# Slot and expert inputs turned for the matrix unit: one 128-column transpose for the last 64 features of two blocks

## Chip, cores and metric

The kernel runs on one core of a Trainium2 chip. The metric is the device time of one execution in microseconds (us): 1408.03 us is the median of three runs (1406.95 to 1409.55). The engines of the core are named as in the profile: PE is TensorE (PEld its weight loads), DVE is VectorE, ACT is ScalarE, POOL is GpSimd, and SP issues most transfers.

## The reference

A small language-model tower over 32 batches of 128 tokens with 192 features: embedding, attention, a soft mixture of 64 experts, attention with 12 heads, and a routed mixture of 8 experts. The change touches the inputs of the two mixtures:

```python
# soft mixture: x is [32, 128, 192], phi_n is [64, 16, 192]
logits = jnp.einsum('bmd,npd->bmnp', x, phi_n)
D = jax.nn.softmax(logits, axis=1)
C = jax.nn.softmax(logits.reshape(bsz, m, n * p), axis=-1)
Xs = jnp.einsum('bmd,bmnp->bnpd', x, D)
hdn = _layernorm(Xs, ln_g[:, None, :], ln_b[:, None, :])
hdn = jnp.einsum('bnpd,ndh->bnph', hdn, w1) + b1[:, None, :]   # h = 384
hdn = jax.nn.gelu(hdn, approximate=False)
Ys = jnp.einsum('bnph,nhd->bnpd', hdn, w2) + b2[:, None, :]
Y = jnp.einsum('bsd,bms->bmd', Ys.reshape(bsz, n * p, d), C)
# routed mixture: 8 experts of 512 tokens, h = 768
h = gelu(jnp.einsum('ecd,edm->ecm', expert_inputs, w1) + b1[:, None, :])
expert_outputs = gelu(jnp.einsum('ecm,emd->ecd', h, w2) + b2[:, None, :])
```

## The kernel before

The program has four phases, one after the other: `tower_phase` (embedding, attention, slot logits and slot sums; 0 to 340 us of the profiled span), `expert_phase` "e0" (the 64 experts of the soft mixture; 340 to 875 us), `combine_phase` (second attention and router; to about 1260 us) and `expert_phase` "e1" (the 8 routed experts; to the end).

Each expert works on 512 rows of 192 features, held as four blocks of 128 rows. The first product contracts over features, so the features must lie on the 128 partitions: PE turns each block with transposes against `ident`. 192 features are one full run of 128 and a rest of 64. The rest is laid out twice side by side (columns `D:` of `rows`, written by a DVE copy after the norm at L1379, or by a second transfer at L220 for the routed experts), so that a full 128-column transpose gives the 64 remaining features twice, in the lower and in the upper 64 partitions. That makes 8 transposes for an expert: four blocks times two.

fp32 operands are split into a high part (rounded to fp32r) and a low part. The high and low parts of the rest are stacked over the two halves of the partitions, `e_x_hi_over_lo`, so that the rest costs two products instead of three. After the transposes, ACT takes both turned banks to `e_x_full` (L1289, two of 128x512) and rounds both (L1295, one of 128x1024); DVE subtracts for the low part of the first 128 features (L1348) and makes the stack with a sign that is 0 in the lower and -1 in the upper half (L1350).

One turn of the e0 loop is, on PE: 15 matmuls of the first product for expert n (three output banks of five, L60 is the helper `matmuls`), the 8 transposes for expert n+2 (L1218), and 12 matmuls of the second product for expert n (L1246). Each fp32 matmul stands in the profile as two records, so the 12 are 24 records. They contract over the three parts of `h_full` in turn, and in the first block of rows PE waits ahead of the first, second and third matmul for the GELU of that part on ACT (L1319, counted by `acted`). On DVE a turn is: split of expert n+1, low part of its weights (L1355), layer-norm statistics of expert n+3 (L1362 to L1369), a wait for POOL's power (L1180), the norm (L1376, four of 128x192), the copy (L1379), and the bias addition of expert n (L1404), which waits for the second product. SP's loads wait for semaphores of these steps. The order on each engine is written out by hand; the waits between engines are semaphores, and nothing is moved by a scheduler. e1 is the same with 30 and 24 matmuls (48 records) for an expert and no layer norm.

In `tower_phase` the same thing is done for 8 groups of four blocks: norm and copy on DVE (L657, L660), four transposes, the rounded part (L787 `x_hi`), the low part (L663), four more transposes (both L962), the rounded rest (L787 `x_rest_hi`), the stack (L667). The turned groups feed the slot logits; the rows themselves, with a leading column of ones, feed the slot sums (L1002), whose column 0 is then the sum of the weights.

## Time and profile before

| | |
|---|---|
| runs | 1406.95, 1408.03, 1409.55 us |
| profiled execution | 1409.95 us, of which the span of its instructions is 1408.2 us |
| busy in the span | PE 95%, PEld 85%, DVE 69%, ACT 66%, POOL 18% |
| granted TensorE clock | 0.986 of full, mean |

The profile is of one execution. "Busy" is the share of the span in which an engine works; "idle before" a group of instructions is the time its engine stood still just ahead of them, with the instruction whose semaphore ended it. Matmuls are pipelined: a record's length holds its latency, and the distance between the starts of neighbours is what one costs.

### The profile page before, as it was taken

Reading aid. Unit: us, or ns where it says so; the run is one execution under the profiler, and the core shown is the slowest. Engines: PE = TensorE matmul, PEld = TensorE weight load, DVE = VectorE, ACT = ScalarE, POOL = GpSimd, SP = SyncE. Lnnn points to the kernel's source line nnn. Section 1 sums busy time; section 2 is a strip of 40 time slices with the busy share of each in tenths; the row PEclk is TensorE's granted clock in tenths of the full one; section 3 lists DMA queues with packets and bytes.
Section 4 is the critical chain, followed back from the end, with each engine's and each line's share of the span. In section 5 each row is a group of like instructions: output and inputs, shape, how many; then the busy total and the mean of one; then the engine's idle time right before and its main releaser. Section 6 shows DMA issues by size and latency. Waiting matters only on the chain. (4 is left out here: it accounts for less than half of the span.)

```text
span 1408.2 us, 29711 instructions
## 1 busy us (share of the span) xinstructions
PE 1332.5 (95%) x9086; PEld 1190.7 (85%) x9086; DVE 971.5 (69%) x2953; ACT 936.1 (66%) x2209; POOL 253.6 (18%) x284
## 2 busy tenths in 40 slices
PE   8799999998999999999999999799999999879995
PEld 6688888886899989998999998688898888768895
DVE  7888877555877777777777773588888888632321
ACT  1488888886666666666666664488888888725551
POOL 5422200001111111111111110012122122111344
PEclk9999999999999999999999999999999999989998
DMA  6144444455666666656665664544454547015631
GB/s 199 45 159 162 162 153 154 157 203 170 196 196 197 186 189 190 200 182 198 190 193 185 193 188 160 160 150 140 154 160 139 152 149 215 15 48 147 158 70 17
DMA packets 181635, 221.04 MB, mean 157 GB/s; under 512 B 25348, under 2 KB 148458, under 8 KB 181536
## 3 DMA queue, kind: packets, MB, share of 16 engines
q1 hardware_dynamic: 147904, 179.52, 41.0%
q10 hardware_dynamic: 25952, 33.32, 7.2%
q0 software_dynamic: 7680, 6.95, 2.7%
q8 instruction: 52, 0.85, 0.3%
q14 instruction: 47, 0.39, 0.1%
HBM read 142.36 MB, written 79.90 MB: 158 GB/s over the span
## 5 line engine op out<-in xcount | busy, mean ns | idle before, releaser
L1246 PE MATMUL bank<-e_w,e_h_full 128*128 128x192 f32 x1920 | 324.7, 326 | 0.4
L1246 PEld LDWEIGHTS bank<-e_w,e_h_full 128*128 128x128 f32 x1920 | 310.6, 190 | 1.7 <-ACT e_h_full L1319 1.3
L1319 ACT ACTIVATE e_h_full<-bank,e_b 128x512 f32<-128x512 f32 x240 | 165.2, 689 | 191.5 <-PE bank L60 191.5
L1180 POOL TENSOR_TENSOR e_ln_rstd<-e_ln_var_eps,minus_half 128x4 f32<-128x4 f32 x62 | 62.5, 1008 | 450.6 <-DVE e_ln_var_eps L1369 450.6
L1727 ACT ACTIVATE probs<-bank,head_neg_max 128x128 f32<-128x128 f32 x384 | 134.9, 393 | 7.6 <-DVE head_neg_max L1823 5.7
L1376 DVE TENSOR_SCALAR e_rows<-e_slot_sums,e_ln_mean_var,e_ln_rstd 128x192 f32<-128x192 f32 x248 | 77.5, 376 | 77.6 <-POOL e_ln_rstd L1180 77.6
L1289 ACT ACTIVATE e_x_full<-bank,e_ln_shift,e_ln_gain 128x512 f32<-128x512 f32 x124 | 89.7, 774 | 44.8 <-PE bank L1218 44.8
L1002 PE MATMUL bank<-x,dispatch_weights 128*128 128x193 f32 x512 | 95.7, 329 | 6.9 <-ACT slot_stage L845 5.9
L60 PE MATMUL bank<-e_x_hi,e_w1hi 128*128 128x512 f32 x216 | 95.4, 442 | 2.3 <-ACT e_h_full L1319 1.2
L1607 PE MATMUL bank<-slot_outputs_then_w_part,combineT 128*128 128x193 f32 x512 | 94.0, 336 | 2.5 <-ACT combineT L1719 2.1
L1404 DVE TENSOR_TENSOR e_stage<-bank,e_b 128x768 f32<-128x768 f32 x64 | 61.3, 957 | 46.5 <-PE bank L1246 46.4
L1607 PEld LDWEIGHTS bank<-slot_outputs_then_w_part,combineT 128*128 128x128 f32 x512 | 84.6, 192 | 9.0 <-issue 9.0
L705 DVE TENSOR_REDUCE column_neg_max<-bank 128x4 f32<-128x512 f32 x64 | 44.2, 690 | 68.5 <-PE bank L60 68.4
L1002 PEld LDWEIGHTS bank<-x,dispatch_weights 128*128 128x128 f32 x512 | 81.9, 190 | 11.0 <-issue 11.0
L1727 ACT ACTIVATION_READ_ACCUMULATOR probs<-bank,head_neg_max 128x1 f32 x384 | 89.2, 232 | 0.0
L823 ACT ACTIVATE slot_exp<-bank,column_neg_max 128x128 f32<-128x128 f32 x256 | 72.9, 373 | 20.2 <-DVE column_neg_max L705 20.2
L60 PE MATMUL bank<-e_x_hi,e_w1lo 128*128 128x512 f32 x216 | 85.3, 395 | 0.0
L60 PE MATMUL bank<-e_x_lo,e_w1hi 128*128 128x512 f32 x216 | 85.2, 394 | 0.0
L60 PE MATMUL bank<-e_x_hi_over_lo,e_w1hi 128*128 128x512 f32 x216 | 85.1, 394 | 0.0
L60 PE MATMUL bank<-e_x_hi_over_lo,e_w1lo 128*128 128x512 f32 x216 | 85.0, 393 | 0.0
L1295 ACT ACTIVATE e_x_hi<-e_x_full 128x1024 fp32r<-128x1024 f32 x70 | 74.0, 1058 | 7.5
L1218 PEld LDWEIGHTS bank<-ident,e_rows 128*128 128x128 f32 x560 | 66.7, 143 | 11.1 <-DMA e_rows<-routed_inputs 1.6
(285 smaller groups left out, 3081.7 us busy)
## 6 DMA issues: line engine op xcount, KB each, us to landing
slot_sums<-slot_stage SPq DMA_DIRECT2D x64, 386.0 KB, 3.2
e_slot_sums<-slot_sums SPq DMA_DIRECT2D x64, 386.0 KB, 3.6
slot_outputs<-e_stage ACTq DMA_DIRECT2D x64, 384.0 KB, 3.2
slot_outputs_then_w_part<-slot_outputs SPq DMA_DIRECT2D x32, 768.0 KB, 4.8
e_w<-in_w SPq DMA_DIRECT2D x64, 288.0 KB, 2.9
slot_logits<-kept_logits SPq DMA_DIRECT2D x32, 512.0 KB, 3.0
slot_logits<-slot_logits SPq DMA_DIRECT2D x32, 512.0 KB, 3.4
e_w1raw<-in_w SPq DMA_DIRECT2D x80, 192.0 KB, 2.7
```

Of the source, the lines that this page charges most:

```text
L60: last = pe.matmul(out, w, m, start=n == 0, stop=n == len(pairs) - 1, **kw)
L823: last = act.activation(ls[:, n % 2, js], logits_bank(n)[:, js], ACT.Exp, bias=nmc[:, n % 2, j:j + 1])
L1002: last = pe.matmul(U[:, j // 2, j % 2, :], disp[:, n % 2, j * P:(j + 1) * P], x3[n // NC % 3][:, j, 0:1 + D], start=True, stop=True)
L1180: pool.tensor_tensor(rs[u][:], ve[u][:], half[:], ALU.pow).then_inc(rstd_ready, 1)
L1218: last = pe.transpose(bank[:, k, j * P:(j + 1) * P], rows[u][:, j, k * P:(k + 1) * P], ident[:])
L1246: last = pe.matmul(ybank(u)[:, j // 2, (j % 2) * D:(j % 2 + 1) * D], hf[:, k, js], w2s[u][:, k, :], start=k == 0, stop=k == MT - 1)
L1289: last = act.activation(xf[:, k, :], bank[:, k, :], ACT.Identity, bias=lnb[:, k, ds(n, 1)], scale=lng[:, k, ds(n, 1)])
L1295: act.activation(xhi[u][:], xf[:], ACT.Copy).then_inc(x_hi_ready, 1)
L1319: act.activation(hf[:, m, :], hbank(u, m), act_fn, bias=b1s[:, m, ds(n, 1)]).then_inc(acted, 1)
L1376: last = dve.tensor_scalar(rows[u][:, j, 0:D], sums[u][:, j, 1:], mv[u][:, j, 0:1], rs[u][:, j:j + 1], ALU.subtract, ALU.mult)
L1607: last = pe.matmul(bank[:, 0, 0:D + 1], cT[:, c, :], ysb[u][:, c, :], start=c == 0, stop=c == NC - 1)
L1727: last = act.activation(pr[:, s, g, :], bank[:, 4 + s, g * P:(g + 1) * P], ACT.Exp, bias=nmx[:, s, g:g + 1], accum_out=esum[:, s, g:g + 1])
```

## The change

For each pair of blocks (even, odd), the rows of the odd block are laid out remaining features first: 64 remaining, then the 128. The even block keeps its order, so the 64 remaining features of the even block and those of the odd one lie side by side, and one 128-column transpose turns both: the even block's land on the lower 64 partitions, the odd block's on the upper. An expert then has 6 transposes: four for the 128 features (`main_of`) and two for the rest (`rest_of`). The bank of the rest is 256 columns wide instead of 512.

The stack of high and low parts is kept, with the halves swapped for odd blocks: ACT rounds the lower half of the rest into the lower half of the stack at even blocks' columns, and the upper half into the upper at odd blocks' columns (`round_rest`, two of 64x256); DVE subtracts into the other halves (`less_rounded`, two of 64x256 that read one half of the partitions and write the other). The duplicate features, the DVE copy and its wait go away. In the tower the norm of an odd block becomes two instructions (128 and 64 features), and the ones of the slot sums move to the last column of an odd block; the stored sums have that layout too, and e0 reads them by `features_of` and `weights_of`. The routed experts' rows come by three transfers instead of two: whole even rows, then the two parts of the odd rows.

```diff
+def main_of(rows, j, first=0):
+    return rows[:, j, first:first + P] if j % 2 == 0 else rows[:, j, DR:D]
+def rest_of(rows, i, first=0):
+    width = first + D
+    return rows[:].rearrange("p j d -> p (j d)")[:, 2 * i * width + first + P:2 * i * width + first + 2 * P]
+def turn_blocks(pe, main, rest, rows, ident, turned):
+    for j in range(GB):
+        last = pe.transpose(main[:, j * P:(j + 1) * P], main_of(rows, j), ident[:])
+    last.then_inc(turned, 1)
+    for i in range(2):
+        last = pe.transpose(rest[:, i * P:(i + 1) * P], rest_of(rows, i), ident[:])
+    last.then_inc(turned, 1)
+def round_rest(act, stacked, rest):
+    two = rest.rearrange("p (i n) -> p i n", i=2)
+    act.activation(even(stacked[0:DR]), two[0:DR], ACT.Copy)
+    return act.activation(odd(stacked[DR:P]), two[DR:P], ACT.Copy)
+def less_rounded(dve, stacked, rest):
+    two = rest.rearrange("p (i n) -> p i n", i=2)
+    dve.tensor_tensor(even(stacked[DR:P]), two[0:DR], even(stacked[0:DR]).bitcast(F32), ALU.subtract)
+    return dve.tensor_tensor(odd(stacked[0:DR]), two[DR:P], odd(stacked[DR:P]).bitcast(F32), ALU.subtract)
...
 def load_rows(self, sp, n, u):
-        sp.dma_start(self.rows[u][:, :, 0:D], x[:, :, TAG:]).then_inc(self.rows_in[u], 16)
-        sp.dma_start(self.rows[u][:, :, D:], x[:, :, TAG + P:TAG + D]).then_inc(self.rows_in[u], 16)
+        sp.dma_start(self.rows[u][:, 0:4:2, :], x[:, 0:4:2, TAG:]).then_inc(self.rows_in[u], 16)
+        sp.dma_start(self.rows[u][:, 1:4:2, DR:], x[:, 1:4:2, TAG:TAG + P]).then_inc(self.rows_in[u], 16)
+        sp.dma_start(self.rows[u][:, 1:4:2, 0:DR], x[:, 1:4:2, TAG + P:]).then_inc(self.rows_in[u], 16)
...
 # expert_phase: PE, ACT, DVE
-                    for k in range(2):
-                        for j in range(4):
-                            last = pe.transpose(bank[:, k, j * P:(j + 1) * P],
-                                                rows[u][:, j, k * P:(k + 1) * P], ident[:])
-                        last.then_inc(turned, 1)
+                    turn_blocks(pe, bank[:, 0, :], bank[:, 1, :], rows[u], ident, turned)
...
-                    act.activation(xhi[u][:], xf[:], ACT.Copy).then_inc(x_hi_ready, 1)
+                    act.activation(xhi[u][:, 0, :], xf[:, 0, :], ACT.Copy)
+                    round_rest(act, xst[u], xf[:, 1, 0:2 * P]).then_inc(x_hi_ready, 1)
...
-                    dve.scalar_tensor_tensor(xst[u][:], f32(xhi[u][:, 1, :]), lo_sign[:, 0:1], xf[:, 1, :],
-                                             ALU.mult, ALU.add).then_inc(x_split, 1)
+                    less_rounded(dve, xst[u], xf[:, 1, 0:2 * P]).then_inc(x_split, 1)
...
-                    Steps(dve, norm_steps, n, 1).link(last)
-                    dve.tensor_copy(rows[u][:, :, D:], rows[u][:, :, P:D]).then_inc(normed, 1)
+                    last.then_inc(normed, 1)
...
 # tower_phase, slot_input: DVE
-                        for j in range(GB):
-                            last = dve.tensor_scalar(xx[:, j, 1:1 + D], hrow(x, j), xmv[:, j, 0:1], xrs[:, j:j + 1],
-                                                     ALU.subtract, ALU.mult)
-                        st.link(last)
-                        dve.tensor_copy(xx[:, :, 1 + D:], xx[:, :, 1 + P:1 + D]).then_inc(x3_ready, 1)
+                        for j in range(GB):
+                            places = ((slice(1, 1 + D), slice(0, D)),) if j % 2 == 0 else (
+                                (slice(DR, D), slice(0, P)), (slice(0, DR), slice(P, D)))
+                            for to, of in places:
+                                last = dve.tensor_scalar(xx[:, j, to], hrow(x, j)[:, of], xmv[:, j, 0:1],
+                                                         xrs[:, j:j + 1], ALU.subtract, ALU.mult)
+                        last.then_inc(x3_ready, 1)
```

PE's queue at the place between the two products of one expert, in the loop of e0, before. A REGISTER_ALU or ISA row that stands between matmuls computes or holds a wait:

```order
L60 MATMUL bank<-e_x_hi_over_lo,e_w1lo 128x512
L1211 REGISTER_ALU
L1054 ISA
L1218 MATMUL bank<-ident,e_rows 128x128 x8
L1238 ISA
L1054 REGISTER_ALU
L1246 MATMUL bank<-e_w_0,e_h_full 128x192
L1245 REGISTER_ALU
L1246 MATMUL bank<-e_w_0,e_h_full 128x192
L1245 REGISTER_ALU
L1246 MATMUL bank<-e_w_0,e_h_full 128x192 x10
```

The same place in the changed kernel (its helpers have other line numbers: L115 is the helper of the products, L91 and L94 are the transposes, L1296 is the second product):

```order
L115 MATMUL bank<-e_x_hi_over_lo,e_w1lo 128x512
L1265 REGISTER_ALU
L1109 ISA
L91 MATMUL bank<-ident,e_rows 128x128 x4
L94 MATMUL bank<-ident,e_rows 128x128 x2
L1288 ISA
L1109 REGISTER_ALU
L1296 MATMUL bank<-e_w_0,e_h_full 128x192
L1295 REGISTER_ALU
L1296 MATMUL bank<-e_w_0,e_h_full 128x192
L1295 REGISTER_ALU
```

Two of eight transposes are gone; the waits stand where they stood.

DVE's queue over one turn of the same loop, before:

```order
L1348 TENSOR_TENSOR e_x_lo<-e_x_full,e_x_hi 128x512
L1350 SCALAR_TENSOR_TENSOR e_x_hi_over_lo<-e_x_hi,minus_upper,e_x_full 128x512
L1355 TENSOR_TENSOR e_w1lo<-e_w1raw,e_w1hi 128x768
L72 ISA
L1362 BN_STATS e_ln_stats<-e_slot_sums 128x6 x4
L1363 SCALAR_TENSOR_TENSOR e_ln_eps_s<-e_slot_sums 128x4
L72 ISA
L1367 BN_AGGR e_ln_mean_var<-e_ln_stats 128x2 x4
L89 REGISTER_ALU
L1369 TENSOR_TENSOR e_ln_var_eps<-e_ln_mean_var,e_ln_eps_s 128x4
L1372 REGISTER_ALU
L1054 REGISTER_ALU
L1376 TENSOR_SCALAR e_rows<-e_slot_sums,e_ln_mean_var,e_ln_rstd 128x192 x4
L1379 COPY e_rows<-e_rows 128x4x64
L1396 ISA
```

And in the changed kernel:

```order
L1399 TENSOR_TENSOR e_x_lo<-e_x_full,e_x_hi 128x512
L108 TENSOR_TENSOR e_x_hi_over_lo<-e_x_full,e_x_hi_over_lo 64x2x128
L109 TENSOR_TENSOR e_x_hi_over_lo<-e_x_full,e_x_hi_over_lo 64x2x128
L1405 TENSOR_TENSOR e_w1lo<-e_w1raw,e_w1hi 128x768
L127 ISA
...
L1427 TENSOR_SCALAR e_rows<-e_slot_sums,e_ln_mean_var,e_ln_rstd 128x192 x4
L1446 ISA
```

One instruction of 128x512 became two of 64x256, and the copy at the end is gone.

## Rows read from the trace of the kernel before

**Rows 1.** The page: engines over the span; granted PE clock in 40 slices, in tenths.
```profile
PE 1332.5 (95%) x9086; PEld 1190.7 (85%) x9086; DVE 971.5 (69%) x2953; ACT 936.1 (66%) x2209; POOL 253.6 (18%) x284
PEclk9999999999999999999999999999999999989998
```

**Rows 2.** Busy time by stretch: e0's loop, tower, e1 (clock, DMA share, GB/s last).
```profile
400.00:800.00 400.00, 400.00 (x2281) 362.71 (x2280) 305.85 (x921) 257.48 (x341) 48.38 (x48) 1.00 0.62 191
130.00:330.00 200.00, 192.60 (x1188) 172.73 (x1187) 136.97 (x354) 169.04 (x424) 21.80 (x21) 1.00 0.48 172
1268.00:1400.00 132.00, 125.02 (x674) 111.96 (x672) 36.18 (x61) 62.25 (x91) 47.63 (x31) 0.99 0.47 103
```

**Rows 3.** Waits, 370 to 830 us: us in total, times, longest.
```profile
DVE e_stage L1404 <- PE bank L1246: 28.1, 54, 0.6
PEld bank L60 <- ACT e_h_full L1319: 8.7, 56, 0.2
```

**Rows 4.** Timeline, one expert in e0's loop: start us, us, engine, line, operation [idle before].
```profile
602.70 0.39 PE L60 MATMUL bank<-e_x_hi_over_lo,e_w1lo 128*128 128x512 f32 x1
602.93 1.04 PE L1218 MATMUL bank<-ident,e_rows 128*128 128x128 f32 x8
603.23 0.69 ACT L1319 ACTIVATE e_h_full<-bank,e_b 128x512 f32<-128x512 f32 x1 [0.46 <-PE bank L60]
603.69 3.88 PEld L1246 LDWEIGHTS bank<-e_w,e_h_full 128*128 128x128 f32 x24
603.80 4.07 PE L1246 MATMUL bank<-e_w,e_h_full 128*128 128x192 f32 x24
609.15 0.69 ACT L1319 ACTIVATE e_h_full<-bank,e_b 128x512 f32<-128x512 f32 x1 [1.24 <-PE bank L60]
```

**Rows 5.** Timeline, expert 62 of e0, which has no transposes.
```profile
857.99 0.74 PEld L1246 LDWEIGHTS bank<-e_w,e_h_full 128*128 128x128 f32 x4
858.41 0.69 ACT L1319 ACTIVATE e_h_full<-bank,e_b 128x512 f32<-128x512 f32 x1 [0.44 <-PE bank L60]
859.15 3.22 PEld L1246 LDWEIGHTS bank<-e_w,e_h_full 128*128 128x128 f32 x20 [0.42 <-ACT e_h_full L1319]
```

**Rows 6.** Timeline, DVE in e0's loop.
```profile
605.85 1.25 DVE L1376 TENSOR_SCALAR e_rows<-e_slot_sums,e_ln_mean_var,e_ln_rstd 128x192 f32<-128x192 f32 x4 [1.30 <-POOL e_ln_rstd L1180]
607.14 0.29 DVE L1379 COPY e_rows<-e_rows 128x256 f32<-128x256 f32 x1
608.88 0.68 DVE L1348 TENSOR_TENSOR e_x_lo<-e_x_full,e_x_hi 128x512 fp32r<-128x512 f32 x1
609.48 0.74 DVE L1350 SCALAR_TENSOR_TENSOR e_x_hi_over_lo<-e_x_hi,minus_upper,e_x_full 128x512 fp32r<-128x512 f32 x1
610.14 0.95 DVE L1355 TENSOR_TENSOR e_w1lo<-e_w1raw,e_w1hi 128x768 fp32r<-128x768 f32 x1
```

**Rows 7.** Groups of ACT by line, whole span: busy us, mean ns, idle before.
```profile
L1295 ACT ACTIVATE e_x_hi<-e_x_full 128x1024 fp32r<-128x1024 f32 x70 | 74.0, 1058 | 7.5
L823 ACT ACTIVATE slot_exp<-bank,column_neg_max 128x128 f32<-128x128 f32 x256 | 72.9, 373 | 20.2 <-DVE column_neg_max L705 20.2
L839 ACT ACTIVATE dispatch_weights<-bank 128x512 f32<-128x512 f32 x64 | 38.8, 605 | 22.7 <-PE bank L995 22.0
```

**Rows 8.** Timeline of the tower: a middle group's second transposes, the last group's logits.
```profile
198.30 0.66 PE L962 MATMUL bank<-ident,x 128*128 128x128 f32 x4 [0.46 <-DVE x_lo L663]
300.13 0.50 PE L60 MATMUL bank<-x_hi,phi_hi 128*128 128x512 f32 x1 [0.29 <-DVE x_hi_over_lo L667]
```

**Rows 9.** Timeline, first experts of e0.
```profile
350.52 1.45 ACT L1289 ACTIVATE e_x_full<-bank,e_ln_shift,e_ln_gain 128x512 f32<-128x512 f32 x2 [4.33 <-PE bank L1218]
354.42 0.50 PE L60 MATMUL bank<-e_x_hi,e_w1hi 128*128 128x512 f32 x1 [1.20 <-ACT e_h_full L1319]
```

**Rows 10.** Timeline, start of e1: a transfer of rows, the first transposes.
```profile
1258.20 0.90 ACTq L220 DMA_DIRECT2D e_rows<-routed_inputs  x1
1263.00 1.97 PE L1218 MATMUL bank<-ident,e_rows 128*128 128x128 f32 x8 [1.16 <-DMA e_rows<-routed_inputs]
```

More of the change, by code:

```diff
@@ L54, in group4, with even, odd, features_of @@
     return ap.rearrange("p (j n) -> p j n", j=GB)
+def even(ap):
+    return group4(ap).rearrange("p (i two) n -> p i two n", two=2)[:, :, 0, :]
+def odd(ap):
+    return group4(ap).rearrange("p (i two) n -> p i two n", two=2)[:, :, 1, :]
+def features_of(rows, j):
+    return rows[:, j, 1 - j % 2:1 - j % 2 + D]
+def weights_of(rows):
+    return rows[:].rearrange("p j d -> p (j d)").rearrange("p (i w) -> p i w", i=2)[:, :, 0:2 * D + 2:2 * D + 1]
+def main_of(rows, j, first=0):
[18 more added lines that the diff above has]
+    return dve.tensor_tensor(odd(stacked[0:DR]), two[DR:P], odd(stacked[DR:P]).bitcast(F32), ALU.subtract)
 def matmuls(pe, out, pairs, **kw):
@@ L192, in __init__ @@
             self.lng, self.lnb = sb("ln_gain", [P, 2, n_exp]), sb("ln_shift", [P, 2, n_exp])
-            self.rows = [sb(f"rows{u}", [P, 4, D + DR]) for u in range(2)]
+            self.rows_wide = [sb(f"rows{u}", [P, 4, D + DR]) for u in range(2)]
+            self.rows = [w[:].rearrange("p j d -> p (j d)")[:, 0:4 * D].rearrange("p (j d) -> p j d", j=4)
+                         for w in self.rows_wide]
             self.xf = sb("x_full", [P, 2, 512])
@@ L210, in __init__ @@
             self.w1lo = [sb("w1lo0", [P, 2, hid], F32R), parts[1]]
-            self.rows = [sb(f"rows{u}", [P, 4, D + DR]) for u in range(2)]
+            self.rows = [sb(f"rows{u}", [P, 4, D]) for u in range(2)]
     def load_sums(self, sp, n, u):
@@ L268, in first_turn @@
         past(pe, self.x_taken, 2 * u)
-        for k in range(2):
-            for j in range(4):
-                last = pe.transpose(banks[k][:, j * P:(j + 1) * P], self.rows[u][:, j, k * P:(k + 1) * P], ident[:])
-            last.then_inc(self.turned, 1)
+        turn_blocks(pe, banks[0], banks[1], self.rows[u], ident, self.turned)
     def first_take(self, act, u, banks):
@@ L276, in first_take @@
             act.wait_ge(self.small_in, 16 * 7)
-        for k in range(2):
+        for k, c in enumerate((4 * P, 2 * P)):
             act.wait_ge(self.turned, 2 * u + k + 1)
             past(act, self.x_split, u)
-            act.activation(self.xf[:, k, :], banks[k], ACT.Identity, bias=self.lnb[:, k, u:u + 1],
+            act.activation(self.xf[:, k, 0:c], banks[k][:, 0:c], ACT.Identity, bias=self.lnb[:, k, u:u + 1],
                            scale=self.lng[:, k, u:u + 1]).then_inc(self.x_taken, 1)
         act.wait_ge(self.x_taken, 2 * u + 2)
-        act.activation(self.xhi[u][:], self.xf[:], ACT.Copy).then_inc(self.x_hi_ready, 1)
+        act.activation(self.xhi[u][:, 0, :], self.xf[:, 0, :], ACT.Copy)
+        round_rest(act, self.xst[u], self.xf[:, 1, 0:2 * P]).then_inc(self.x_hi_ready, 1)
     def first_w1_hi(self, act):
@@ L385, in tower_phase @@
         vector_steps = sem("vector_steps")
-        typed, xn = sb("typed", [P, GB, D]), small.rows[0]
+        typed, xn = sb("typed", [P, GB, D]), small.rows_wide[0]
         st6, mv = sb("ln_stats", [P, GB, 6]), sb("ln_mean_var", [P, GB, 2])
@@ L408, in tower_phase @@
         xve, xrs = sb("x3_var_eps", [P, GB]), sb("x3_rstd", [P, GB])
-        x3 = [sb(f"x3_{k}", [P, GB, 1 + D + DR]) for k in range(3)]
-        xhi1 = sb("x_rest_hi", [P, 512], F32R)
+        x3 = [sb(f"x3_{k}", [P, GB, 1 + D]) for k in range(3)]
         xvar, xrstd, x3_ready = sem("x3_var_ready"), sem("x3_rstd_ready"), sem("x3_ready")
@@ L806, in evict @@
                     if s == 4 and x is not None:
-                        past(act, x_split, x)
-                        take(x3T_done, 2 * x + 2, xhi1[:], b5, x_hi_took)
+                        past(act, logits, NC * (x - 1))
+                        act.wait_ge(x3T_done, 2 * x + 2)
+                        round_rest(act, T["x_hi_over_lo"][x % 2], b5[:, 0:2 * P]).then_inc(x_hi_took, 1)
                     if s == 4 and a is not None:
@@ L960, in turn_x3 @@
                         pe.wait_ge(x_lo_ready, x + 1)
-                    for j in range(GB):
-                        last = pe.transpose(b5[:, j * P:(j + 1) * P], x3[x % 3][:, j, 1 + k * P:1 + (k + 1) * P],
-                                            ident[:])
+                    for j in range(GB if k == 0 else 2):
+                        last = pe.transpose(b5[:, j * P:(j + 1) * P], (main_of, rest_of)[k](x3[x % 3], j, 1), ident[:])
                     last.then_inc(x3T_done, 1)
@@ L1281, in take_x @@
                 def take_x(n, u):
-                    for k in range(2):
+                    for k, c in enumerate((4 * P, 2 * P)):
                         act.wait_ge(turned, 2 * n + k + 1)
@@ L1286, in take_x @@
                         if ln is None:
-                            last = act.activation(xf[:, k, :], bank[:, k, :], ACT.Copy)
+                            last = act.activation(xf[:, k, 0:c], bank[:, k, 0:c], ACT.Copy)
                         else:
-                            last = act.activation(xf[:, k, :], bank[:, k, :], ACT.Identity,
+                            last = act.activation(xf[:, k, 0:c], bank[:, k, 0:c], ACT.Identity,
                                                   bias=lnb[:, k, ds(n, 1)], scale=lng[:, k, ds(n, 1)])
```

42 lines of the change are left out of this document (19 added, 23 removed).

## The prediction

> **What bounds the kernel now.** I read the page first: PE is busy 95% of the span, DVE 69%, ACT 66%, and the granted clock is near full throughout [rows 1]. A mean share hides the stages, so I read busy time by stretch next: in e0's loop (400 to 800 us) PE is busy in all 400.00 us at clock 1.00, in the tower 192.60 of 200 us, in e1 125.02 of 132 us [rows 2]. A busy record is not work at peak, so the waits come third: between 370 and 830 us no PE matmul waits at all; only its weight loads wait 56 times, up to 0.2 us, ahead of a first-product bank [rows 3]. DVE waits for PE at every bias addition, 28.1 us over 54 of them, 0.52 us each [rows 3]. So in e0 PE sets the pace and DVE has half a microsecond to spare. Last, the timeline of one expert [rows 4] gives the prices: the eight transposes start at 602.93 and the second product at 603.80, so one costs 0.87/8 = 0.109 us. The second product has 24 records in 3.9 us and the first product 15 matmuls of 0.23 us; 3.46 + 0.87 + 3.9 = 8.23 us is one expert, with no gap.
>
> **e0, PE.** Two transposes fewer: 0.219 us an expert, if nothing else is late. What is late next is the GELU of the third part of h. It hangs on the end of the first product, not on the transposes, which only cover it. The last first-product matmul starts at 602.70; ACT ends that GELU at 603.92, 1.22 us later [rows 4]. Expert 62 has no transposes and shows what needs it [rows 5]: four weight loads go ahead, the fifth waits until 859.15, 0.05 us after ACT's end (858.41 + 0.69 = 859.10). The fifth load opens the third matmul, as the waits in PE's queue stand. With eight transposes the second product's loads begin at 603.69, and the fifth is due 0.6 us later (0.11 to the second load, then 0.163 a record), at 604.29; it may start from 603.97. The slack is 0.32 us; I take away 0.219 and 0.10 is left. So the whole 0.219 counts. Of the 64 experts 62 have transposes in e0's loop; the first of these belongs to the start-up below: 61 x 0.219 = **13.4 us** (12.5 if the slack of 0.10 is used up by jitter now and then).
>
> One rule would price this otherwise. The record of a transpose is 0.27 us long (the group of eight ends 1.04 us after its start, seven pitches of 0.109 and one record) [rows 4]. The Trainium skill, "TensorE: Matmul & The Clock Gate", Part 4: PE-mode transpose, gives about 275 ns for a 128x128 transpose within a kernel, mostly access latency. Taken as the price, two would be 0.55 us an expert and e0's term 33 us. The record agrees with that figure, the distance between starts (0.109) doesn't, and the queue is paid by the distance.
>
> **e0, DVE.** The copy of 0.29 us and the wait ahead of it go (the norm ends at 607.10, the copy at 607.43): -0.33 us. The stack of 128x512 costs 0.66 us from start to next start (609.48 to 610.14) and becomes two of 64x256 on half the partitions, which no row shows. Bounds for one: 0.29 us (the 256-wide copy) and 0.68 us (the 512-wide subtraction) [rows 6]. The 512-wide takes 0.68 and the 768-wide 0.95 us, 1.05 ns an element, so 256 wide is about 0.42 us; with the overlap of 0.08 us that neighbours show (0.68 long, next start after 0.60) two are 0.68: +0.02 us. DVE's wait becomes 0.52 + 0.33 - 0.02 - 0.219 = 0.6 us. Even at the upper bound, with no overlap at all (1.36 us, +0.70), the wait would shrink to about -0.07, that is, PE would lose that and keep 0.15 us an expert.
>
> A rule speaks against the change here. The two subtractions read one half of the partitions and write the other. The Trainium skill, "VectorE: DVE Perf Modes", section "Two Vector instructions with no wait between them", says that an instruction whose start quadrant differs from that of the last input or output is held until all earlier ones have finished. By it the two and the one behind them lose their overlap, 3 x 0.08 = 0.24 us; the wait would be 0.37 instead of 0.6 us, and the sum would not change. No row of before has such a pair back to back.
>
> **e0, ACT.** It takes 256 columns less (the taking of the rest), and the rounding of 1024 in 1.06 us becomes one of 512 and two of 64x256; 512 takes 0.60 and 128 0.37 us [rows 7], a slope of 0.6 ns a column, so 256 is about 0.45 (the bounds are 0.37 and 0.60, for half the partitions and crossed columns too, which no row shows). At 0.60 + 0.45 + 0.45 less two overlaps of 0.1 the rounding grows by about 0.2 us, and the taking shrinks by 0.2. ACT waits 1.24 us for the next first product [rows 4]; nothing comes of it.
>
> **Start-up of e0.** PE waits 1.20 us at 354.42 for ACT, whose run began at 350.52 when the first transposes of the phase were done [rows 9], which themselves waited for the copy. Copy gone 0.33, narrower taking 0.2, rounding back 0.2: **0.3 us** (0 to 0.5). The end of the tower, where the first two experts are prepared by the same chain, gains the same 0.3 and pays up to 0.4 for split and rounding twice: **0.1** (-0.3 to 0.5).
>
> **Tower.** Eight groups lose two transposes each. They stand behind a wait for DVE's low part (0.46 us at 198.30 [rows 8]), whose chain is itself started by PE's earlier logits, so the shift passes through: 0.219 each. In the first group PE has other waits. In the last, PE waits 0.29 us at 300.13 for the stack [rows 8]; DVE's side may grow by 0.02 to 0.26 us, which takes the gain. Six count: **1.3 us** (0 to 1.5). The norm goes from four instructions, a wait and a copy to six instructions; DVE is not late there.
>
> **e1.** Six of eight experts turn rows inside the loop, PE has no wait to speak of: 6 x 0.219 = **1.3 us**. At the start PE waits for the rows [rows 10]. A third transfer queues behind the one issued from 1258.20 to 1259.10: 0.6 to 0.9 us later, also for what stands behind on ACT and SP and for the end of the phase, though a quarter fewer bytes move. The 8 transposes there take 1.97 us (0.24 each, the clock is at its lower level, 1.2 GHz), so two fewer are worth 0.48 on the way to ACT. I take **0.2 us** gained (-0.9 to 0.9).
>
> **Sum.** 13.4 + 0.3 + 0.1 + 1.3 + 1.3 + 0.2 = 16.6 us. The profiled execution took 1409.95 us (span 1408.2) and would take 1393.35; it lies 1.9 us over the median, so against the median of 1408.03 it is **1391.4 us**.
>
> **Rivals.**
> - The cover of the GELU is gone, and a wait takes the place of the transposes. If all parts of h were needed at the first load of the second product, that load could not come before 603.97 and e0 would gain nothing but start-up effects: 1408 - 3.2 = 1404.8. [Rows 5] speak against it: four loads went ahead. 4%.
> - DVE becomes the bound, but not past the old pace: the half-height pair costs 1.3 to 1.5 us, where DVE's wait (0.52 + 0.33 + 0.66 - 0.219 = 1.29 us, less the pair) is used up. At 1.5 e0 keeps 0.01 us an expert; 1392 to 1404. The slope of [rows 6] is against it. 5%.
> - Slower: the same pair costs more than 1.5 us (0.66 + 0.33 + 0.52) and the old wait is used up too. From there each further 0.1 us is on every turn: at 1.0 us an instruction the loop is 8.23 + 0.49 us, 61 x 0.49 = 30 us, less 3 elsewhere: 1435. Nothing shows a crossed half to cost over twice a full one. 2%.
> - Transposes cost their record: 13.4 becomes 33, about 1371. Starts are against it. 2%.
>
> **Numbers.** The forecast has 87%. Its own range: tower 0 to 1.5, start-ups -1.2 to 1.9, e0 12.5 to 13.4, and 1.3 us of run-to-run either way give 1388.5 to 1396. I leave the rest out, so the range is 1388.5 to 1396.0. No change means within 0.2% (2.8 us), about what a measurement can tell: faster 96% (the first rival just counts there), same 1.5%, slower 2.5%.
>
> **What would show it.** e0 at 8.02 us an expert, PE still without matmul waits, no wait of the second product for ACT (the slack of 0.10), DVE's wait before the bias addition near 0.4 to 0.6 us; about 140 fewer PE records; first rows of e1 landing within 1 us of before. Wrong would be a PE wait for ACT between the products, or DVE's wait at zero.

## The result

In the series of this comparison the changed kernel took 1401.01 us (median of 5 runs, 1397.28 to 1401.54), the kernel before 1409.55 us (median of 5, 1406.95 to 1411.06). The ratio is 0.9925, 95% interval 0.9911 to 0.9938, that is 10.6 us less (8.7 to 12.5). This ratio is the record's own estimate and not the quotient of the two medians, which lie 8.5 us apart (0.9939). The forecast was 1391.4 us with a range that ended at 1396.0: the kernel became faster by the mechanism that was named, but by a third less than the 16.6 us of the forecast. A second series of the changed kernel gave 0.9903 (0.9888 to 0.9919), 13.7 us less, with medians 12.4 us apart (1399.15 against 1411.5). The profiled execution took 1397.63 us, span 1395.9 us; the one of before 1409.95 and 1408.2.

The page, engines and granted clock, to be held against [rows 1]:
```profile
PE 1320.4 (95%) x8926; PEld 1175.0 (84%) x8926; DVE 974.7 (70%) x2977; ACT 951.6 (68%) x2361; POOL 253.5 (18%) x284
PEclk9899999999999999999999999999999999989998
```
There are 160 matmul records fewer (about 140 were forecast; two transposes at each of 64 experts of e0, two of which are turned at the end of the tower, of eight groups of the tower and of eight experts of e1 are 160). ACT has more instructions and more busy time; PE's share stays at 95%. The windows of e0's loop and of the tower, in the columns of [rows 2]:
```profile
400.00:800.00 400.00, 400.00 (x2235) 359.88 (x2234) 311.31 (x940) 273.39 (x448) 49.82 (x50) 1.00 0.64 196
130.00:330.00 200.00, 192.45 (x1179) 172.42 (x1179) 140.16 (x369) 171.66 (x437) 21.40 (x21) 1.00 0.48 173
```
PE is still busy in all of e0's 400 us. Waits, 370 to 830 us, as [rows 3]:
```profile
DVE e_stage L1454 <- PE bank L1296: 19.2, 57, 0.4
PEld bank L115 <- ACT e_h_full L1370: 11.2, 57, 0.2
```
Two things are to be seen. DVE's wait at the bias addition shrank from 0.52 to 0.34 us (19.2/57), where 0.6 was forecast. And the weight loads' wait for the first GELU grew, from 8.7 to 11.2 us in about as many experts. That second row explains the miss in e0's loop. In the kernel before it was read as harmless, and there it was.

Two neighbouring experts in e0's loop, beside [rows 4] (start us, us, engine, line, operation, idle before):
```profile
604.73 0.69 ACT L1370 ACTIVATE e_h_full<-bank,e_b 128x512 f32<-128x512 f32 x1 [0.87 <-PE bank L115]
605.46 0.19 PEld L115 LDWEIGHTS bank<-e_x_hi,e_w1hi 128*128 128x128 f32 x1 [0.23 <-ACT e_h_full L1370]
606.73 0.60 PE L91 MATMUL bank<-ident,e_rows 128*128 128x128 f32 x4
607.03 0.69 ACT L1370 ACTIVATE e_h_full<-bank,e_b 128x512 f32<-128x512 f32 x1 [0.52 <-PE bank L115]
607.17 0.38 PE L94 MATMUL bank<-ident,e_rows 128*128 128x128 f32 x2
607.28 3.88 PEld L1296 LDWEIGHTS bank<-e_w,e_h_full 128*128 128x128 f32 x24
607.38 4.07 PE L1296 MATMUL bank<-e_w,e_h_full 128*128 128x192 f32 x24
612.73 0.69 ACT L1370 ACTIVATE e_h_full<-bank,e_b 128x512 f32<-128x512 f32 x1 [0.76 <-PE bank L115]
613.48 0.19 PEld L115 LDWEIGHTS bank<-e_x_hi,e_w1hi 128*128 128x128 f32 x1 [0.16 <-ACT e_h_full L1370]
```
The six transposes run from 606.73 to the first matmul of the second product at 607.38: 0.65 us, 0.109 each as forecast, against 0.87 for eight. The second product's 24 loads take 3.88 us without a wait, as before, so the cover over the last GELU holds. What is new is the first GELU. In the turn at 604.73 it starts 0.87 us after ACT's last work, in the next turn (612.73) after 0.76; the load of the third bank, which needs it, waits 0.23 and 0.16 us. The wait of 0.16 us costs nothing: the load comes 0.344 us after the one ahead of it and the next follows 0.109 later, 0.453 us for what two steps of 0.231 take elsewhere. The wait of 0.23 us makes it 0.42 + 0.11, and 0.07 us is lost. In the distance from one second product to the next (58 steps from the fourth expert on) the turns alternate between 8.086 and 8.014 us (medians), mean 8.049. Before they stood at 8.244 and 8.232, mean 8.238.

DVE in the same turns, beside [rows 6]:
```profile
603.49 0.96 DVE L1454 TENSOR_TENSOR e_stage<-bank,e_b 128x768 f32<-128x768 f32 x1 [0.38 <-PE bank L1296]
604.36 0.68 DVE L1399 TENSOR_TENSOR e_x_lo<-e_x_full,e_x_hi 128x512 fp32r<-128x512 f32 x1
605.06 0.42 DVE L108 TENSOR_TENSOR e_x_hi_over_lo<-e_x_full,e_x_hi_over_lo 64x256 fp32r<-64x256 f32 x1
605.49 0.42 DVE L109 TENSOR_TENSOR e_x_hi_over_lo<-e_x_full,e_x_hi_over_lo 64x256 fp32r<-64x256 f32 x1
605.95 0.96 DVE L1405 TENSOR_TENSOR e_w1lo<-e_w1raw,e_w1hi 128x768 fp32r<-128x768 f32 x1
```
A subtraction on half the partitions takes 0.42 us, the value taken from the slope. None of the three starts behind the first overlaps its forerunner (604.36 + 0.68 = 605.04, next start 605.06), where before 0.08 us was overlapped. From the low part to the split of w1 it is 1.59 us against 1.26 before (608.88 to 610.14 in [rows 6]).

ACT's groups over the whole span, beside [rows 7] (busy us, mean ns):
```profile
L1345 ACT ACTIVATE e_x_hi<-e_x_full 128x512 fp32r<-128x512 f32 x70 | 44.2, 631 | 7.5
L102 ACT ACTIVATE e_x_hi_over_lo<-e_x_full 64x256 fp32r<-64x256 f32 x72 | 29.8, 414 | 0.8
L101 ACT ACTIVATE e_x_hi_over_lo<-e_x_full 64x256 fp32r<-64x256 f32 x72 | 28.9, 401 | 0.0
```
The halves take 401 and 414 ns, within the bounds of 0.37 and 0.60 us that were set for them, and the 512 columns 631 ns.

The tower's last group, where [rows 8] had a wait of 0.29 us at 300.13:
```profile
299.48 0.68 DVE L737 TENSOR_TENSOR running_max<-running_max,kept_logits 128x512 f32<-128x512 f32 x1
300.19 0.42 DVE L108 TENSOR_TENSOR x_hi_over_lo<-bank,x_hi_over_lo 64x256 fp32r<-64x256 f32 x1
300.62 0.43 DVE L109 TENSOR_TENSOR x_hi_over_lo<-bank,x_hi_over_lo 64x256 fp32r<-64x256 f32 x1
301.10 0.50 PE L115 MATMUL bank<-x_hi,phi_hi 128*128 128x512 f32 x1 [0.52 <-DVE x_hi_over_lo L109]
```
The wait is 0.52 us now. From the first to the last slot sums of the tower it takes 257.21 us (257.93 before). A second loss lies in the third group, where DVE starts a column maximum late without waiting for anything that the profile shows:
```profile
153.62 0.69 DVE L760 TENSOR_REDUCE column_neg_max<-bank 128x4 f32<-128x512 f32 x1 [0.26 <-issue]
```
The third group takes 35.07 us where its neighbours take 34.73, and 34.93 before, where the same instruction overlapped its forerunner (start at 151.94, the forerunner from 151.86 to 152.03).

Start of e1, beside [rows 10]:
```profile
1245.66 0.60 ACTq L276 DMA_DIRECT2D e_rows<-routed_inputs  x1
1247.21 0.63 ACTq L278 DMA_DIRECT2D e_rows<-routed_inputs  x1
1250.59 1.11 PE L91 MATMUL bank<-ident,e_rows 128*128 128x128 f32 x4 [0.65 <-DMA e_rows<-routed_inputs]
1251.49 0.63 PE L94 MATMUL bank<-ident,e_rows 128*128 128x128 f32 x2
```
Three transfers instead of two, and yet the rows are there 4.93 us after the first issue (1245.66 to 1250.59); before it was 5.43 us (first issue at 1257.57). The six transposes end 1.53 us after their start, where eight took 1.97. The gain does not reach the first second product of e1 in this execution: from the first issue to there it takes 19.74 us (19.04 before), with the clock granted at its lower level (1.2 GHz) for 10.2 us of it, from 1249.8 us on, against 6.8 us before.

### The profile page after: what moved, and what is told of

It is laid out like the page before. It is cut to its first block and busy times, and to the rows that moved or that the text cites. A ratio compares the mean times of both kernels' runs of the same rounds, so it can differ in the third digit from the quotient of the medians.

```text
span 1395.9 us, 29574 instructions
## 1 busy us (share of the span) xinstructions
PE 1320.4 (95%) x8926; PEld 1175.0 (84%) x8926; DVE 974.7 (70%) x2977; ACT 951.6 (68%) x2361; POOL 253.5 (18%) x284
## 5 line engine op out<-in xcount | busy, mean ns | idle before, releaser
L1296 PE MATMUL bank<-e_w,e_h_full 128*128 128x192 f32 x1920 | 324.7, 326 | 0.4
L1296 PEld LDWEIGHTS bank<-e_w,e_h_full 128*128 128x128 f32 x1920 | 310.6, 190 | 1.7 <-ACT e_h_full L1370 1.3
L1339 ACT ACTIVATE e_x_full<-bank,e_ln_shift,e_ln_gain 128x512 f32<-128x512 f32 x124 | 76.5, 667 | 42.9 <-issue 37.6
L115 PE MATMUL bank<-e_x_hi,e_w1hi 128*128 128x512 f32 x216 | 98.0, 454 | 2.7 <-ACT e_h_full L1370 1.7
L1057 PEld LDWEIGHTS bank<-x,dispatch_weights 128*128 128x128 f32 x512 | 82.3, 190 | 11.2 <-issue 11.2
L115 PE MATMUL bank<-e_x_hi_over_lo,e_w1hi 128*128 128x512 f32 x216 | 86.0, 398 | 0.0
L115 PE MATMUL bank<-e_x_hi,e_w1lo 128*128 128x512 f32 x216 | 85.5, 396 | 0.0
L115 PE MATMUL bank<-e_x_lo,e_w1hi 128*128 128x512 f32 x216 | 85.4, 396 | 0.0
L115 PE MATMUL bank<-e_x_hi_over_lo,e_w1lo 128*128 128x512 f32 x216 | 85.1, 394 | 0.0
L1602 POOL TENSOR_TENSOR ln_rstd<-ln_var_eps,minus_half 128x1 f32<-128x1 f32 x64 | 35.9, 561 | 211.0 <-DVE ln_var_eps L1942 153.8
L122 PE MATMUL bank<-spare_operand 128*128 128x512 f32 x229 | 64.1, 428 | 8.4 <-PEq L1558 4.2
```

The costliest lines, as they stand in the source:

```text
L115: last = pe.matmul(out, w, m, start=n == 0, stop=n == len(pairs) - 1, **kw)
L122: pe.matmul(out, T["spare"][:, 0:P], T["spare"][:], start=True, stop=True)
L1057: last = pe.matmul(U[:, j // 2, j % 2, :], disp[:, n % 2, j * P:(j + 1) * P], x3[n // NC % 3][:, j, 0:1 + D], start=True, stop=True)
L1296: last = pe.matmul(ybank(u)[:, j // 2, (j % 2) * D:(j % 2 + 1) * D], hf[:, k, js], w2s[u][:, k, :], start=k == 0, stop=k == MT - 1)
L1339: last = act.activation(xf[:, k, 0:c], bank[:, k, 0:c], ACT.Identity, bias=lnb[:, k, ds(n, 1)], scale=lng[:, k, ds(n, 1)])
```

## The experiments

All times of a loop or stretch below are read as above: from the start of one second product to the next, or from slot sums to slot sums. In the series of the first four kernels before took 1411.5 us, in the second four 1410.79, in the last three 1412.7.

**The changed kernel again.** No edit.

> The changed kernel once more, nothing edited. Its first profile (span 1395.9 us) starts the first slot sums 1.73 us later than before, in instructions that the change leaves alone, and its five runs lie at 1397.3 to 1397.6 and at 1401.0 to 1401.5 us. Theory A (where PE's clock drops and when an instruction arrives late differ from run to run): this profile starts the slot sums at another time, by 1 us or more, and the loop of e0 keeps its pace (8.013 and 8.087 us in turn). Theory B (the changed code causes the late start): the first slot sums start at 73.1 us within 0.2 us again.

Measured: 1399.15 us, ratio 0.9903 (0.9888 to 0.9919). e0's loop 8.117 and 8.023 us, mean 8.065; tower 257.09; e1 107.49. The alternation of the turns is there again. The first slot sums start at 72.06 us, 1.06 us earlier than in the first profile: Theory A.

**Eight transposes in e0.** The rest is turned twice, the second time over the first; everything else stays as changed.
```diff
-    for i in range(2):
+    for i in rests:                # (0, 1, 0, 1) in e0, (0, 1) in e1
```

> The changed kernel, but e0's loop turns the two pairs of the rest twice (same output), so PE has eight transposes an expert again while ACT and DVE work as changed. Forecast's theory (e0's gain is PE's two transposes and nothing else): an expert takes 8.23 to 8.24 us again, the run is about 61 x 0.19 = 11 to 13 us slower than the changed kernel, and DVE's wait ahead of the bias addition is about 0.19 us longer than in it (0.33 to 0.52). Rival (the removed copy and the narrower taking brought part of the gain): an expert stays under 8.20 us.

Measured: 1413.19 us, ratio 1.0006 (0.9996 to 1.0016). The medians of the run and of the changed kernel beside it are 14.0 us apart (11 to 13 forecast). e0's loop is 8.276 us, 0.21 to 0.23 more than with six; the whole gain of the changed kernel goes with these two transposes, and the rival falls. But 8.276 is 0.04 more than before (8.238), with the same number of transposes. So the rest of the edit costs 0.04 us an expert by itself, 2.3 us in 61 experts. The waits of the weight loads for the first GELU say where:
```profile
PEld bank L115 <- ACT e_h_full L1370: 11.9, 56, 0.3
```

**Eight transposes in the tower.** The rest is turned twice in all eight groups of the tower.

> The changed kernel, but the tower turns the rest of each group with four transposes again (the two, each twice). Forecast's theory: each of the middle groups of the tower takes 0.219 us longer than in the changed kernel, the last group nothing, 1.3 us in all. Rival (the tower is bound by ACT and DVE there, since the changed kernel gained only 0.7 us between the first and the last slot sums): under 0.5 us.

Measured: tower 258.66 us against 257.21 and 257.09, 1.5 us more; the whole kernel 1400.76 us, ratio 0.9917 (0.9901 to 0.9932), not to be told from the changed kernel. The price in the tower is as forecast: each of the first seven groups takes 0.18 to 0.22 us longer than in the changed kernel, the last nothing. Against the kernel before, with as many transposes, it is 0.7 us more (257.93), of which 0.35 us is in the third group and 0.24 in the seventh, whose end holds the last group's logits. So in the tower, too, the rest of the edit has a price of its own.

**Four no-operations for ACT.** Ahead of ACT's first work in each pass of the expert loop:
```diff
+                        if u == 0 and not isinstance(n, int):
+                            for _ in range(4):
+                                act.nop(nofuse=True)
```

> The changed kernel with four empty instructions on ACT at the head of each pass of e0's loop, ahead of the rounding of w1. In the changed kernel every second expert takes 8.087 instead of 8.013 us: the first GELU of the pass starts 0.14 us after its register instruction, elsewhere 0.06, and PE waits for it at the third bank. Theory A (the instruction comes late to ACT after the jump back, by where it lies in the code): moving it changes the pattern, and both turns take 8.01 us, 2.2 us less in all, or the late one moves elsewhere. Theory B (ACT is behind in its own work, since its run ends 0.36 us later than before): four empty instructions leave 8.087 as it is or make it longer.

Measured: 8.026 and 8.027 us, mean 8.025; the alternation is gone: Theory A. Over 61 experts that is 2.4 us less than in the changed kernel run beside it (8.065) and 1.5 us less than in its first profile (8.049). ACT starts its first GELU after 0.77 and 0.74 us:
```profile
603.72 0.69 ACT L1373 ACTIVATE e_h_full<-bank,e_b 128x512 f32<-128x512 f32 x1 [0.77 <-PE bank L115]
611.75 0.69 ACT L1373 ACTIVATE e_h_full<-bank,e_b 128x512 f32<-128x512 f32 x1 [0.74 <-PE bank L115]
```
and the waits of the weight loads are back where they were before the change:
```profile
PEld bank L115 <- ACT e_h_full L1373: 8.9, 56, 0.3
```
In the whole kernel nothing is seen of it: 1398.83 us, ratio 0.9901 (0.9884 to 0.9919), as without the edit. Its profiled execution spent 412.93 us in the combine phase, those of the three runs above 408.3 to 411.8. Here and below, the combine phase is the stretch from the last second product of e0 to the first of e1.

**The kernel before again.** No edit.

> The kernel before, unchanged, for a second profile of it. The question is the spread of the stretches that the change does not touch. If the later first slot sums of the changed kernel (73.1 and 72.1 us against 71.4) and the longer half-clock stretch around 339 us (6.8 against 3.4 us) belong to the change, this profile repeats before: first slot sums near 71.4, last slot sums to the first second product of e0 17.4 us, combine phase 410.6. If they are chance, it differs from the first profile of before by up to 2 us in one of them. In either case: e0's loop 8.238 us an expert, last minus first slot sums 257.9, e1 108.5, ratio 1.000.

Measured: 1411.93 us, ratio 1.0005 (0.999 to 1.002). First slot sums at 72.13 us (71.40 in the first profile of before), combine phase 412.37 (410.64), e0's loop 8.233, tower 257.96, e1 108.55. In all 13 profiles the first slot sums start between 71.2 and 73.1 us and the combine phase takes 407.0 to 413.1 us; the loops repeat to some hundredths of a microsecond. The granted clock says what goes with the combine phase: it is at its lower level for 10.2 us where the phase takes 407.0 us, for 13.7 us at 407.9 and 408.2, 17.1 at 408.3 and 409.1, 20.5 at 409.6 to 410.6, 23.9 at 411.8 to 412.9, and 27.3 at 412.4 and 413.1. Kernels before and changed lie in both halves of that list. For the head it is less clear. The first slot sums start at 71.2, 71.4 and 72.1 us in three profiles of the old code and at 71.3 to 73.1 us, mean 72.2, in ten of the changed one. One kernel alone moved by 1.06 us between two profiles, so the 1.7 us between the first profiles of before and changed don't show a loss by the change; that some tenths belong to it is not excluded.

**Four transposes in e0.** The remaining 64 features are not turned at all from the third expert on.
```diff
-    for i in range(2):
+    for i in range(2 if rest is not None else 0):     # None in e0 from expert 2 on
```

> From expert 2 on, e0 does not turn the remaining 64 features at all (left out of the computation: each expert uses what stands in that bank), four transposes instead of six; nothing else changes. Theory A (the slack of the GELU cover that is left after the change is 0.10 us, as worked out from the timelines of before): the fifth weight load of the second product now waits for ACT, and an expert takes 8.05 - 0.219 + 0.12 = about 7.95 us, 6 us less in all, ratio to before about 0.988. Rival B (no such limit, the price of 0.109 us a transpose goes on): 7.83 us, 13 us less in all, ratio 0.983. Rival C (DVE bounds first: its wait of 0.35 us shrinks by 0.22 only, so it should not): DVE's wait for the second product at zero.

Measured: 1386.73 us, ratio 0.9826 (0.9802 to 0.9849). e0's loop 7.929 and 7.858, mean 7.892: between the two forecasts. The groups of weight loads of the second product, 370 to 820 us, with the idle time before them last; four transposes first, then the changed kernel:
```profile
L1298 PEld LDWEIGHTS bank<-e_w,e_h_full 128*128 128x128 f32 x1369 | 219.6, 190 | 4.9
```
```profile
L1296 PEld LDWEIGHTS bank<-e_w,e_h_full 128*128 128x128 f32 x1342 | 216.8, 190 | 0.0
```
Now there is a wait inside the second product. It stands before the fifth load: 0.276 us from the fourth to the fifth, 0.108 to the sixth, where two steps of 0.163 would be; that is 0.058 us lost, and 8.049 - 0.219 + 0.058 = 7.888. Theory A was right on what comes next, and the slack that the changed kernel has left is 0.219 - 0.058 = 0.16 us, not 0.10. Rival B would have had 7.83, with no wait there. DVE did not bound: it still waits 10.1 us over 53 experts.

**The last group of the tower.** In slot 4 of the last group DVE subtracts before it takes the running maximum.
```diff
+                    early = s == 4 and x == NG - 1
+                    if early:
+                        slot_input(x, s)
                     if n1 is not None:
                         running_max(n1)
```

> Changed kernel, but in the last group of the tower DVE does the two small subtractions of the stack before the running maximum that stood ahead of them. Theory: the gap of 0.52 us in PE at 301 us was the stack arriving late behind that maximum, so it goes to 0.1 us or less and last minus first slot sums takes 256.7 instead of 257.1 to 257.2 us. Rival: PE then waits for the maximum, or for another step of the same chain, and the time stays at 257.1. In the whole time 0.4 us cannot be seen: ratio as the changed kernel's, 0.990 to 0.9925.

Measured: tower 256.62 us, and the gap is gone:
```profile
298.24 0.42 DVE L109 TENSOR_TENSOR x_hi_over_lo<-bank,x_hi_over_lo 64x256 fp32r<-64x256 f32 x1
298.70 0.69 DVE L737 TENSOR_TENSOR running_max<-running_max,kept_logits 128x512 f32<-128x512 f32 x1
298.72 0.50 PE L115 MATMUL bank<-x_hi,phi_hi 128*128 128x512 f32 x1
```
PE no longer idles ahead of the logits, 0.5 to 0.6 us are gained (0.4 forecast). Whole kernel 1395.46 us, ratio 0.9895 (0.987 to 0.992).

**More idle-bank matmuls at the end of the tower.**
```diff
-                keep_busy(pe, T, bank[:, 6, :], 4)
+                keep_busy(pe, T, bank[:, 6, :], 12)
```

> Changed kernel with 12 instead of 4 idle-bank matmuls ahead of the transpose of the token maxima. Theory: the idle gap of 2.28 us at 338 us brings on the half-clock stretch, which lasted 6.8 us in two of three profiles and there stretches the first products of e0; filled, the stretch is 3.4 us or gone, and from the last slot sums to the first second product takes 15.5 to 16.5 us instead of 17.4. Rival: half-clock stretches come whether the gap is filled or not, 17 to 17.5 us. Whole time: at most 1.5 us less, which the ratio (0.990 expected, 0.989 to 0.9925) hardly shows.

Measured: 15.12 us from the last slot sums to the first second product, below the forecast of 15.5 to 16.5, against 17.43 in the changed kernel run again, 16.22 in its first profile. First the changed kernel (first profile), then this one:
```profile
338.53 0.40 PE L1098 MATMUL bank<-ident,token_neg_max 128*32 128x128 f32 x1 [2.28 <-DVE token_neg_max L766]
341.65 0.63 PE L115 MATMUL bank<-e_x_hi,e_w1lo 128*128 128x512 f32 x1
```
```profile
337.35 0.28 PE L1098 MATMUL bank<-ident,token_neg_max 128*32 128x128 f32 x1 [0.44 <-DVE token_neg_max L766]
339.98 0.40 PE L115 MATMUL bank<-e_x_hi,e_w1lo 128*128 128x512 f32 x1
```
PE's idle gap here is longer than in the kernel before, where all three profiles have the same 1.43 us; all eight of the changed code with four such matmuls have 2.27 or 2.28:
```profile
337.97 0.28 PE L1043 MATMUL bank<-ident,token_neg_max 128*32 128x128 f32 x1 [1.43 <-DVE token_neg_max L711]
```
In the first profile of the changed kernel PE was idle for 2.28 us and the clock was granted at its lower level (1.2 GHz) from 338.4 us for 6.8 us; a matmul of e0's first product takes 0.63 us there. With the gap filled there is no such stretch and it takes 0.40. But before had none either in its second profile (15.27 us there) and one of 3.4 us in its first (15.98 us), and the changed kernel with no-operations elsewhere (below), whose gap is 2.28 us too, had none and took 15.34 us. Of eleven profiles with the gap open nine have a stretch of 3.4 or 6.8 us, of two with it filled none. So filling it most likely avoids the stretch, worth up to 2 us when it comes; it is not shown that the change brought it on. Whole kernel 1395.58 us, ratio 0.9896 (0.9873 to 0.9919).

**The no-operations in the kernel before.** The edit of the fourth run, on the old code.

> The kernel before, with 4 no-operations at the head of ACT's pass of the expert loop, the same edit that took the changed kernel's e0 from 8.065 to 8.025 us an expert. Theory A (the late first GELU of every second turn came in with the changed ACT code, whose instructions after the jump arrive late; before had none of it): e0's loop stays at 8.24 us an expert, ratio 1.000 (0.998 to 1.002). Rival B (before pays for the jump too, and the no-operations help any kernel with this loop): 8.20 us an expert, 2.5 us less, ratio 0.998.

Measured: 1411.6 us, ratio 1.0 (0.9988 to 1.0013), e0's loop 8.271 and 8.229, mean 8.250. Nothing gained, 0.01 us an expert lost: before had no late first GELU to cure. Theory A. So the lateness came with the changed code.

**The no-operations in the second turn of the pass.** The same with `u == 1`; this kernel has a single timed execution (1400.49 us), so only its loop is read.

> The changed kernel with the 4 no-operations at the head of the second turn of each pass of ACT's loop instead of the first. Theory A (what is late is the first instructions behind the jump, so only instructions ahead of the first GELU help): turns still alternate, 8.08 to 8.12 and 8.02 us, mean 8.05 to 8.065. Rival B (it is where the loop's code lies in memory as a whole, and any four instructions more shift it): both turns at 8.02 to 8.03 us.

Measured: 8.087 and 8.013 us, mean 8.048, the changed kernel's pace; the waits of the weight loads are the changed kernel's too:
```profile
PEld bank L115 <- ACT e_h_full L1373: 11.2, 57, 0.2
```
Four instructions more in the loop do nothing by themselves; they help ahead of the first GELU. Theory A. One rival stays open: in the fourth run they also shift the place of that GELU in the code, and no run shifts it by instructions ahead of the loop. So "time between the jump and the GELU" and "place of the GELU in the code" are not told apart.

**The three edits together.**

> The changed kernel with three edits together: the 4 no-operations at the head of ACT's loop pass, the last group's two small subtractions ahead of the running maximum, and 12 instead of 4 idle-bank matmuls ahead of the transpose of the token maxima. If the three gains add up: e0's loop 8.025 us an expert (2 us less in all), slot sums 256.6 to 256.7 us (0.4 less), from the last slot sums to the first second product of e0 near 15.1 us (1 to 2 less): 3.5 to 4.5 us under the changed kernel, that is a ratio to before of 0.9865 to 0.989. Rival (they hide each other, or a half-clock stretch comes elsewhere in their place): 0.990.

Measured: 1394.21 us, ratio 0.9875 (0.9853 to 0.9898), 17.7 us less than before. e0's loop 8.017 us, tower 256.49, last slot sums to first second product 14.97 us. In the profile each of the three stretches has the time that its edit gave alone, so the gains add up there. The whole kernel is faster than before; its interval lies below that of the change alone in the first series (0.9911 to 0.9938) and just overlaps that of the second (0.9888 to 0.9919).

## Why the prediction was wrong, step by step

- **What bounds the kernel**: right. PE paces e0; two transposes put back take the whole gain away (1.0006).
- **Price of a transpose**: right. 0.109 us by distance, not 0.27 by record; 0.211 to 0.227 us for the pair between the runs with eight and six. The rival of 33 us fell.
- **e0, 13.4 us**: this is the step of the mechanism that failed, and the term that was mis-sized most. It held that 0.219 us an expert comes through if nothing else is late, and it looked for lateness only at the last GELU. There the slack was 0.16 us, better than the 0.10 that was worked out. But with the changed code ACT started its first GELU of every second turn some 0.08 us later, where PE's cover is used up to the last hundredth: the waits of [rows 3] (8.7 us over 56, 0.155 us each) were just what PE can hide between two loads, and I took "up to 0.2 us" for harmless without asking how much more would still be. Measured: 61 x (8.238 - 8.049) = 11.5 us, 1.9 less. With the no-operations it is 61 x (8.238 - 8.025) = 13.0, in the last kernel 61 x (8.238 - 8.017) = 13.5: the term as forecast. Why the GELU comes late in the changed code stays open.
- **DVE in e0**: price right (0.42 us), wait 0.34 us rather than 0.6. No overlap is left between the low part, the two halves and the split of w1, +0.33 us a turn. That agrees with the hold that the Trainium skill describes, "VectorE: DVE Perf Modes", section "Two Vector instructions with no wait between them": the prediction's working by that rule had a wait of 0.37 us. As was said there, it didn't change the sum.
- **ACT in e0**: widths and durations right, "nothing comes of it" wrong, by the above.
- **Tower, 1.3 us**: 0.7 measured (257.93, 257.96, 257.88 before; 257.21, 257.09, 257.22 after). The transposes' price is right (1.5 us when put back). The loss is in the last group, where the forecast counted a gain of nothing and 0.2 us was lost, and in the late column maximum of the third group, 0.35 us. That one is no accident of one execution: DVE's 0.26 us without a cause in the profile stands at this instruction in the changed code's profiles and in none of before, and the third group takes 35.03 us or more in all of them (34.93 or less before). Like the late GELU, it is an instruction that came late with the changed code, and why is open. Putting the subtractions first gave 0.5 us back.
- **e1 loop, 1.3 us**: 1.1 from its first to its last second product (108.53 to 107.42), five of the six steps; the sixth lies in the start.
- **e1 start, 0.2 us**: about 0.5, but not in every execution. The third transfer cost nothing, the rows came 0.5 us sooner (4.92 to 5.12 us after the first issue in ten profiles, 5.41 to 5.69 in three of before). From that issue to the first second product it is 18.5 to 18.7 us in six profiles of the changed code, 19.0 to 19.3 in the three of before, and 19.7 to 19.8 in the other four, the first among them, where the clock is at its lower level for 10.2 us around there and not for 3.4 or 6.8. There 0.7 us is lost, near the bound of 0.9, though not by the transfer.
- **Start of e0 and end of the tower, 0.4 us**: from the last slot sums to the fourth expert's second product 43.73 and 43.91 us in the two profiles of before, 43.52 and 44.71 in the two of the changed kernel and 43.50 with the no-operations in the second turn. The spread covers the term; it stays open.

The measured terms are 11.5 + 0.7 + 1.1 + 0.5 = 13.8 us, 2.8 less than the forecast sum, and would have given 1394.2, still inside the range. What put the time outside it is the last term, the 1.3 us that the range allowed for runs either way. It failed in two ways. The base of 1408.03 us was the median of three runs, and the kernel before then had medians of 1409.55, 1411.5, 1410.79 and 1412.7 us in four series, with single runs from 1406.8 to 1415.7. And the changed kernel's medians in its two series are 1401.01 and 1399.15. The bounds of the range also add up to 1396.7, not to the 1396.0 that was stated.

The two series say 10.6 (8.7 to 12.5) and 13.7 us. The second agrees with the terms. The 3 us that the first lacks are in none of the loops, as far as its one profile shows. They can be put down in part to the clock: its five runs were granted 0.978 to 0.985, mean 0.982, where the kernel before had a mean of 0.985 in each of three later series of 17 runs (of its runs in the first series only one has a clock on record, 0.986). As the two levels are 1.2 and 2.4 GHz, that is about 50 us at the lower level against 42. Within those series of before a microsecond more at the lower level goes with 0.26 to 0.34 us more time, so an estimate from these numbers is 2 to 3 us. This is a correlation. Whether the change itself brings more time at the lower level is open: in its second series it was 45 us.

## What to carry to other kernels

A wait that costs nothing now has a length up to which it costs nothing: work out that length, and how near the present wait is to it, for each handover between the two engines, not only for the one that the edit uncovers. Price an instruction that stands in a full queue by the distance between starts, and take loops from the traces, which here repeat to two hundredths, while the whole time wanders by several microseconds. Size the range of a whole time by more than three runs. Where a loop is paced by handovers and its turns suddenly alternate, look at the first instruction behind the jump.

## What had not been expected of the hardware

- Counted from the start of the matmul that completes its bank, the first GELU behind the loop's backward jump starts after 0.604 us in the changed code (median over 400 to 800 us; 0.614 in its second run), after 0.526 in the other turn (0.535), 0.524 in both turns of before, and 0.529 with four no-operations ahead of it. The same four in the second turn leave it at 0.604. Why the old code had no such delay, at the same place in the loop, stays open.
- Instructions on half the partitions cost what their width says, and half the partitions save nothing: 0.42 us on DVE for 64x256, as the slope of the full-height rows gave, and 0.40 and 0.41 on ACT, where the full-height rounding of 1024 columns (1058 ns before) and of 512 (631 ns after) comes to 0.42 us for 256.
- The combine phase, whose code no kernel here changes but for the start of e1 at its end, varies by 6 us between executions (407.0 to 413.1 us), in step with the time that its clock is granted at the lower level (10.2 to 27.3 us), while the expert loop's turns, at full clock throughout, repeat to 0.02 us. What PE did ahead of each of these stretches was not looked into.
